# Products of zeros ahead of five waits of TensorE in a mixer, experts, deformable convolution and routed FFN kernel

## The reference

```
x = x + mixer(ln(x))     # t = xW; y = relu(xn xn^T)^2 t over all 3136 tokens of the image
x = x + experts(ln(x))   # 16 experts of 128 hidden, softmax gate, the two best weighted:
                         #   sum_e disp[e] * (silu(x w1_e) * (x w2_e)) w3_e
x = x + dcn(ln(x))       # 3x3 convolution at learned offsets: gather 4 corners, weigh, multiply
x = x + route(ln(x))     # the better half of the tokens by x wr: gelu(x f1 + b1) f2 + b2, times x wr
```

## Time and profile before

| | |
|---|---|
| median of 3 runs | 4599.6 us (4589.32 to 4605.0) |
| span of the profiled execution, first to last instruction | 4742.8 us; no other time of that execution is given |
| TensorE matmul | 3689.9 us busy (78%), 21912 instructions |
| DVE, ACT, POOL | 3096.6 (65%), 2394.1 (50%), 1954.9 (41%) us busy |
| mean granted TensorE clock | 0.858 |

### The profile page before, as it was taken

One profiled execution on the slowest core, in us unless ns is written; L12 is line 12 of the kernel. 1 busy time (PEld: TensorE's weight loads), 2 busy tenths in 40 slices (PEclk: granted clock), 3 DMA queues, 4 the chain that ended last, 5 costly groups with the idle time before them and its releaser, 6 DMA issues.

```text
span 4742.8 us, 58643 instructions
## 1 busy us (share of the span) xinstructions
PE 3689.9 (78%) x21912; PEld 1953.7 (41%) x21912; DVE 3096.6 (65%) x4834; ACT 2394.1 (50%) x4144; POOL 1954.9 (41%) x1805
## 2 busy tenths in 40 slices
PE   6889868888788878889788888889788888864432
PEld 2334434444444444444444444444544444433421
DVE  5466457766677566766577567766577576664765
ACT  5656644466445654466445664456444664431210
POOL 0000344526255343535255353544345354446661
PEclk8999979999799978999799888989799988975555
DMA  3000222222122221222122221231222222233436
GB/s 99 8 1 1 73 59 60 65 66 79 51 65 68 70 72 57 67 73 71 51 65 66 70 77 55 64 86 51 55 71 72 71 71 57 60 89 89 111 97 125
DMA packets 374811, 314.93 MB, mean 66 GB/s; under 512 B 312672, under 2 KB 317024, under 8 KB 374528
## 3 DMA queue, kind: packets, MB, share of 16 engines
q0 software_dynamic: 85248, 231.33, 16.5%
q1 hardware_dynamic: 289280, 79.88, 7.9%
HBM read 279.30 MB, written 57.69 MB: 71 GB/s over the span
## 4 chain that ended last, share of the span: by engine, by line
PE 54%; DVE 14%; ACT 9%; another core or an unknown queue 9%; issue 7%; DVEq 3%; DMA 2%; POOL 2%; SPq 1%; ACTq 0%
PE PS L1487 49%; DVE work L866 3%; PE PS L1690 3%; DVEq L488 2%; ACT work L1379 2%; DVE G L492 2%; POOL G L448 2%; PE PS L1522 1%; ACT work L1308 1%; DVE G L486 1%; DVE st L454 1%; DVE small L862 1%; DVE work L777 1%; DMA out<-x 1%
## 5 line engine op out<-in xcount | busy, mean ns | idle before, releaser
L448 POOL DMA_INDIRECT G<-corner_table,index x1800 | 1954.3, 1086 | 2651.6 <-DVE value L494 1256.1
L1379 ACT ACTIVATE work<-PS,descale 128x512 f32<-128x512 f32 (+2 forms) x896 | 565.5, 633 | 638.0 <-PE PS L1487 510.6
L866 DVE SCALAR_TENSOR_TENSOR work<-PS,descale,work 128x512 f32<-128x512 f32 (+2 forms) x896 | 604.8, 681 | 385.0 <-ACT work L1379 276.1
L1308 ACT ACTIVATE work<-PS 128x768 f32<-128x768 f32 (+2 forms) x800 | 650.5, 823 | 374.3 <-PE PS L1487 251.0
L777 DVE TENSOR_TENSOR work<-work 128x768 f32<-128x768 f32 (+2 forms) x496 | 481.1, 973 | 440.2 <-PE PS L1487 280.3
L1487 PE MATMUL PS<-xn_hl,xn_hh 128*128 128x384 f16 (+2 forms) x1600 | 550.8, 345 | 121.8 <-ACT work L1308 76.3
L1487 PE MATMUL PS<-work,xm 128*64 128x400 f32 (+3 forms) x3200 | 642.1, 514 | 0.4 <-DVE work L777 0.4
L486 DVE TENSOR_TENSOR G<-G,corner_w 128x768 f32<-128x768 f32 x600 | 559.8, 951 | 55.9 <-DMA G<-corner_table,index 53.4
L1487 PE MATMUL PS<-xn_hl,xn_ll 128*128 128x384 f16 (+2 forms) x1600 | 546.7, 342 | 0.0
L1487 PE MATMUL PS<-work,w3s 128*64 128x384 f32 (+2 forms) x1792 | 466.8, 600 | 85.6 <-DVE small L862 80.8
L1487 PE MATMUL PS<-xn_hl,w1h 128*128 128x512 f16 (+2 forms) x896 | 331.1, 370 | 157.5 <-DVE work L866 131.3
(11 more groups left out here) (258 smaller groups left out, 4959.1 us busy)
## 6 DMA issues: line engine op xcount, KB each, us to landing
G<-corner_table,index POOLq DMA_INDIRECT x1800
corner_table<-rows_scratch SPq DMA_DIRECT2D x32, 784.0 KB
corner_table<-G SPq DMA_DIRECT2D x8, 841.0 KB, 8.5
xin<-x SPq DMA_DIRECT2D x8, 768.0 KB, 5.3
rows_scratch<-xln SPq DMA_DIRECT2D x8, 768.0 KB
x_scratch<-xB SPq DMA_DIRECT2D x8, 768.0 KB
yw_scratch<-yw SPq DMA_DIRECT2D x7, 784.0 KB
x<-x_scratch SPq DMA_DIRECT2D x4, 784.0 KB
```

Source lines behind the costliest of these rows:

```text
L448: GP.indirect_dma_start(G[0:rows, n % 2, tap * 4 * C:(tap + 1) * 4 * C], None, tables[b % 2], bass.IndirectOffsetOnAxis(ap=index[0:rows, c ...
L866: V.scalar_tensor_tensor(hid[:, e % 4, 0:w], S[2 + e % 2][:, 0:w], descale[:, MOE2:MOE2 + 1], silu[:, e % 2, 0:w], ALU.mult, ALU.mult).the ...
L1308: A.activation(relu[0:rows, u % 2, :, 0:n], PS[u % 2][0:rows, :, 0:n], ACT.Relu).then_inc(s["relu_done"], 1)
L1379: A.activation(silu[:, e % 2, 0:w], S[e % 2][:, 0:w], ACT.Silu, scale=descale[:, MOE1:MOE1 + 1]).then_inc(s["silu_done"], 1)
```

## The change

A helper `keep_warm(bank, n)` issues n matmuls of zeros by zeros: 128 by 128 stationary, 400 columns moving, each overwriting columns 0 to 399 of a PSUM bank. It is called at five places of TensorE's order: with 8 before the wait for `z_ready` at the end of each half of each image (bank D1); and in images 2 to 7, into bank S[3], with 16 between `ffn_up` and `ffn_down` of the first FFN chunk, with 8 after that `ffn_down`, with 24 before the wait for `sm_shift`, and with 24 before the wait for `disp_split`. No semaphore is added, and no other instruction is moved or removed.

```diff
+            def keep_warm(bank, n):
+
+                for _ in range(n):
+                    mm(bank[:, 0:max(IWS)], zero16[:, 0:128], zero16[:, :])
...
                     if k >= 2 and half:
                         pe.wait_ge(s["f_cm"], (k - 1) * NCH)
+                    keep_warm(D1, 8)
                     pe.wait_ge(s["z_ready"], k * 2 + half + 1)
...
                     pe.wait_ge(s["x1_added"], 4 * (k + 1))
                     ffn_up(k - 2, 0)
+                    keep_warm(S[3], 16)
                     ffn_down(k - 2, 0)
+                    keep_warm(S[3], 8)
...
                 if k >= 2:
+                    keep_warm(S[3], 24)
                     pe.wait_ge(s["sm_shift"], k + 1)
                     ffn_rest(k - 2, 1)
                     pe.wait_ge(s["gelu_done"], (k - 1) * 2 * NCH)
+                    keep_warm(S[3], 24)
                 pe.wait_ge(s["disp_split"], k + 1)
```

## The result

The changed kernel took 4645.75 us in the median (4618.43 to 4650.05), the kernel before 4589.32 on the same chip: ratio 1.0113, interval [1.0085, 1.0140], slower by 1.1% or some 52 us. The forecast was 4601 us, the range ended at 4642. Chips differ, as it seems (the three jobs of the experiments ran on three): the kernel before took 4585 and 4589 us in two jobs and 4713 and 4717 us in two others. Its trace ahead of the prediction (span 4742.8) is like those of the second kind, the trace after (span 4648.2, with a run time of 4650.05) is of the first, so these two spans are not compared.

What follows compares the result with a forecast made beforehand. TensorE paces the mixer; between mixer and experts a chain of waits from engine to engine, at clock 0.64, does. Terms: 2.9 - 7.3 + 0 + 3.5 - 12.3 + 24.5 - 9.7 = +1.6 us, so 4601 us, range 4566 to 4642.

Steps and rivals of the forecast that it cites:

- rival B: Block before the wait for `disp_split` stays on the path and buys nothing: +34.4, 4634 us; chance 0.22.
- First halves (+2.9): Ends of first halves: 1.36 us of zeros in a 0.87 us wait, +0.49 us in six halves, +2.9 us.
- Nothing hides it: End of a first half: the +0.49 us overrun counts, since the second half waits for the y products' addition.
- Second halves (-7.3): Ends of second halves: zeros fit the wait, y products gain 1.83 us each, at most 14.6; half taken, -7.3 us.
- something other than the products' speed: End of second halves: what holds DVE's second addition, starting 2.9 us after the last y product; so half the gain taken.
- 16, 8 and 24 (0 and +3.5): Blocks around `ffn_down` cost 0; the 24 before `sm_shift` overrun 0 to 1.16 us in six images, half taken, +3.5.
- the recording's: Wait for `sm_shift`: DVE's late start, 9 of 11 us odd, may be partly due to recording the profile.
- `ffn_rest` (-12.3): Stage after the gate: 24.6 us excess over full clock in six images; zeros before `sm_shift` save half, -12.3 us.
- Last block (+24.5): 24 zeros before the already met wait for `disp_split`: on the path, 4.08 us in each of six images, +24.5.
- Experts' first products (-9.7): Experts' start: 4.86 us at clock 0.50, 14.6 us excess in six images; two thirds saved, -9.7 us.
- Rival A: Clock holds, all three savings come in full, block before `sm_shift` stays hidden: -26.4, 4573 us; chance 0.25.
- Rival C: Zeros do not raise the clock, every block met at half clock costs its long price: +112, 4712 us; chance 0.07.

Runs made afterwards that it cites:

- third job: On one chip, kernel before 4713.33 us: 48 zeros before `disp_split` alone 1.0104; change without last block 1.0006; whole change 1.0049; zeros at second halves plus moved work 0.9944.
- first job: On one chip, kernel before 4716.92 us: itself again 0.9994; change without last block 0.9992; last block alone 1.0064; only the 8 products at the halves' ends 1.0006.
- second job: On one chip, kernel before 4584.53 us: whole change 1.0091; one gather without zeros 0.9050, with all blocks but the last 0.9012; moved work alone 0.9994.
- moved work: Kernel before with the router's 56 products and the second FFN chunk's up products issued before the wait for `sm_shift`, no zeros: 4577.29 us, 0.9994.
- one gather: Kernel before issuing one of a tile's nine gathers, convolution not computed: 4145.57 us, 0.9050; the same with all blocks of zeros but the last: 4130.75 us, 0.9012.
- zeros at one place and moved work: Kernel before plus 8 zeros at ends of second halves only, and the moved work before the wait for `sm_shift`: 4687.95 us, 0.9944.

## Why the prediction was wrong

The forecast was a balance of gains and costs within 0.3%; the time came 1.1% above. The median lies 4 us past the range, whose upper end had been set to take in rival B; taken against the median that it was set from (4642 of 4599.6, 1.0092) that end is inside the measured interval.

In the timed runs both sides of the balance came out slow. Without the last block and what it buys the forecast sums to -13.2 us; timed, -4 [-19, 11] and +3 [-8, 14]. The last block with what it buys was put at +14.8; timed, 30 [13, 48] alone, and 20 in the third job as the difference of two runs. Each miss by itself is near the noise, the whole (23 to 52 us for 1.6) is not. On the kind of chip of the result no run without the last block was timed, so half of its 52 us stays without a timed cause. The step that failed is the one that the gains ahead of the last block rest on: that DVE and ACT follow TensorE's products at the distances of the first trace, or nearer. They follow them at a time that the gathers set. The terms below are read from single traces, for images 2 to 7:

**First halves (+2.9).** By the traces this term is far off. The overrun of the zeros was right (0.57 us more to the y products, for 0.49), but "Nothing hides it" took DVE's addition to follow the products at a fixed distance. In image 5 of the third job it follows 3.7 us later still, and the stretch costs +26.4 us (first job, on one chip, +26.2). In the second job it takes 52.9 us in the change and 37.5 in the kernel with the moved work alone. No run took out these blocks alone, and no timed run shows this cost: with the blocks at the halves alone the stretch is 22.7 us longer, that from second half to dispatch 5.8 shorter (363.7 us), and the time +3 us [-10, 16].

**Second halves (-7.3).** The products' gain came, 10.5 us in six images. The doubt about the addition was right: it is "something other than the products' speed", the same lateness, and in image 4 it starts 4.03 us after the products, for 2.86. How much of the gain this took over all images, 1 us or 8, depends on which trace of the kernel before is set beside it.

By the Trainium skill, "TensorE: Matmul & The Clock Gate", section "Why this matters for your kernels", idle time between bursts of matmuls is to be avoided, since the clock falls by it. The trace agrees on the clock (1.00 in image 4, for 0.61 in the earlier trace rows); the time did not follow it.

**16, 8 and 24 (0 and +3.5).** In the trace after, the block before `sm_shift` ran over only in image 6, by 2.0 us (with one gather in all six, in five by the same amount), so +2.0. What was put down as perhaps "the recording's" was wrong: the run with the profile takes its span and 1.85 us, and with one gather the 9 us vanish. They are of the gathers.

**`ffn_rest` (-12.3).** Not had. In the trace after it is +23.2; in the four others with these blocks the six windows sum to 125.8 to 152.6 us, for 132.2 in the kernel before of the first job. The clock did start full, but where the stage began earlier, among the gathers, the wait of 5 us for the first gelu took the clock down again; where it began with the round over (four images of the change's trace in the third job) it took 17.7 to 18.4 us. The earlier trace rows showed this before: image 6, the only one with GpSimd busy inside, was the longest. What the stage lost had been won ahead of it: from the end of the second half to the first dispatch transpose the change without its last block takes 347.4 and 364.6 us in two traces, the kernel before 369.5. That is -4.9 (same job) and -22.1 (across jobs), around the -16.1 that these terms sum to.

**Last block (+24.5).** On the path, as said; mis-sized, 35.6, because much of it ran at half clock, behind the router's products. The timed difference, where it stood alone, is 30 us [13, 48].

**Experts' first products (-9.7).** Measured 6 x 4.86 less 19.57, so -9.6, as forecast. The timed runs don't contradict it: alone the block costs 30 us for 34.4 of distance, doubled 49 for 59.5.

Put together with the measured sizes: 26.4 for the first halves, -4.9 to -22.1 to the dispatch, 35.6, -9.6, so +30 to +48, against 23, 42 and 52 us timed. This agreement proves little. Without the last block the same reading gives +21.3 and +4.3 us in the two traces, for -4 and +3 timed; the first halves cost more in the traces of the first and third jobs, though the whole loses least in the third. And the sum leaves out the stretch from the experts' first products to the end of the next first half, which takes 1867.4 us in the kernel before of the first job and 1818.4 in the change of the third. Rival B named the outcome and the place, but not for its reason: the clock was raised at all three places, and the block did buy its share. Without the gathers the forecast's sum holds: there, without the last block, forecast 2.9 - 16.1 = -13.2, measured -14.8 us. That is in part luck, since two terms differ and cancel: the y products of second halves save 14.8 us there in six images, and the block before `sm_shift` costs 13. Rival A, with full savings and without that block, would give 2.9 - 14.6 - 24.6 = -36.3. Rival C is out: zeros raise the clock.

Open: what in the gathers holds TensorE up (GpSimd's instructions or their transfers; both went together here), whether its semaphores come late or its instructions run late, why 0.6 us later in a round costs 4.4 us on one kind of chip, and why the loss is twice as large on the other kind, of which no trace of the kernel before exists.

## What to carry to other kernels

A block of zeros ahead of a wait that was already met lay on the path here with its whole length (5.9 us an image), so put such blocks only where the trace shows TensorE idle for longer than the block takes at the clock that it will meet. Before counting a faster stage as time won, look at what follows it: if the next engine starts microseconds after the last product, with "remote" as the releaser, the stage's speed may not be what it waits for. Time each place by itself: here zeros at one place and moved work gained 0.56%, where zeros at five places lost 0.49% in the same job. And see in the trace how fast work runs where it was moved: the router's products took 11 us in the wait for 3 behind it, and moved alone they gained nothing.

## What the runs showed of the hardware

While GpSimd issues indirect gathers, other engines start late after TensorE's products: 9 us at the gate, 4 us at the additions, 3.6 us at the gelu; with one gather of nine 0.03 us at the first two. At the gate of the kernel before the start came 2.0 us after the round's last gather in five of six images. Eight matmuls more ahead of the y products made it 7.69 us for 3.98 in image 5 (third job; 8.36 in the first). TensorE's own small products run slowly there too: 56 of one column took 11 us, for 3.0 where no gather ran. Products of zeros raise the clock and hold it: y products behind 8 of them ran at 1.00 for 0.61 in image 4, and after 24 behind the logits (4.23 us) `ffn_rest` began at full clock. Behind the router's products of one column, 24 zeros took 5.69 us for 4.08, at a granted clock of 0.70.
